# A depthwise and involution kernel: earlier prologue jobs, spare identity products on TensorE, fewer mirror DMAs and a last quarter summed in PSUM

## What is computed

```python
def _gn(v, G=32):                 # groups of two neighbouring channels: mean 0, variance 1
    ...
def _L0_conv_ref(x, ...):         # x is _gn(x)
    h = sign(x)
    h = depthwise_conv3x3(h, sign(dw_weight))
    h = sign(_bn(_prelu(h, prelu1_a), ...))
    h = einsum('bchw,oc->bohw', h, sign(pw_weight))
    return _bn(_prelu(h, prelu2_a), ...) + x
def _L1_conv_ref(x, W, b):        # x is _gn(x)
    filters = einsum('bchw,oc->bohw', x, W) + b      # 9 x 64 filters per pixel
    return sum over the 9 taps of (x shifted by the tap) * (its filter)
x = x + _L0_conv_ref(_gn(x), ...)
x = x + _L1_conv_ref(_gn(x), W, b)
```

## Time and profile before

| what | value |
|---|---|
| median of 3 runs | 772.26 us |
| the profiled execution, own time | 772.17 us |
| its span, first to last instruction | 770.3 us |
| VectorE (DVE) busy | 686.5 us, 89% |
| GpSimd (POOL) busy | 629.7 us, 82% |
| TensorE (PE) busy | 614.4 us, 80% |
| ScalarE (ACT) busy | 491.7 us, 64% |
| HBM read and written | 26.03 MB and 25.69 MB |

### The profile page before, as it was taken

How to read it: one execution, slowest core, us unless ns; L and a number is a source line. 1 busy time by engine, 2 the same in 40 slices (tenths; PEclk the granted TensorE clock), 3 DMA queues, 4 the chain that set the end, 5 groups by cost and what they waited for, 6 DMA issues and landing times.

```text
span 770.3 us, 18752 instructions
## 1 busy us (share of the span) xinstructions
PE 614.4 (80%) x7977; PEld 252.9 (33%) x7977; DVE 686.5 (89%) x988; ACT 491.7 (64%) x614; POOL 629.7 (82%) x421
## 2 busy tenths in 40 slices
PE   0628869888898989888898979888898988898880
PEld 0313324333342433343333423333333433332210
DVE  4346969999998989999998989999999989999998
ACT  5544877676857686776858586777868576725000
POOL 1030595989898898989899899989899899999996
PEclk9857999999999999999999999999999999999996
DMA  5206588898988889898988889898989887897982
GB/s 191 79 1 168 90 178 197 169 237 179 236 189 202 199 192 251 174 237 174 225 202 209 196 189 249 185 239 173 244 178 228 190 190 152 186 189 149 203 173 85
DMA packets 39683, 142.10 MB, mean 184 GB/s; under 512 B 4784, under 2 KB 12976, under 8 KB 37680
## 3 DMA queue, kind: packets, MB, share of 16 engines
q0 software_dynamic: 17136, 75.87, 53.6%
q1 hardware_dynamic: 22436, 65.04, 26.1%
q10 hardware_dynamic: 28, 0.00, 0.0%
HBM read 26.03 MB, written 25.69 MB: 67 GB/s over the span
## 4 chain that ended last, share of the span: by engine, by line
POOL 55%; DMA 19%; issue 9%; DVE 8%; ACT 4%; PE 4%; ACTq 1%; SPq 0%; POOLq 0%
DMA prod<-prod 18%; POOL prod L352 11%; POOL prod L346 11%; POOL ob L361 9%; POOL prod L319 6%; POOL prod L339 5%; POOL prod L331 4%; DVE prod L807 4%; POOL prod L328 4%; POOL st L306 2%; PE dw_ps L447 2%; ACT ab L497 1%; POOL st L304 1%; PE tap_ps L427 1%; ACT unused L497 1%
## 5 line engine op out<-in xcount | busy, mean ns | idle before, releaser
L427 PE MATMUL tap_ps<-q,w_t 64*64 64x392 f32 x2304 | 484.5, 509 | 51.8 <-DMA mirror<-q 20.4
L807 DVE SCALAR_TENSOR_TENSOR prod<-tap_ps,bias,q 128x784 f32<-128x784 f32 x480 | 474.6, 1026 | 35.4 <-PE tap_ps L427 32.9
L427 PE MATMUL tap_ps<-mirror,w_t 64*64 64x392 f32 x2304 | 478.2, 509 | 0.0
L427 PEld LDWEIGHTS tap_ps<-q,w_t 64*64 64x64 f32 x2304 | 149.3, 133 | 271.7 <-DVE prod L807 184.5
L497 ACT ACTIVATE ab<-dw_ps,col 128x784 bf16<-128x784 f32 x128 | 121.0, 995 | 97.7 <-PE dw_ps L447 97.7
L346 POOL TENSOR_TENSOR prod<-prod 128x784 f32<-128x784 f32 x63 | 135.4, 2150 | 9.1 <-DMA prod<-prod 9.1
L361 POOL TENSOR_TENSOR ob<-prod 128x784 f32<-128x784 f32 x63 | 142.2, 2258 | 0.2 <-POOL prod L352 0.2
L447 PE MATMUL dw_ps<-signs,dw_diag 64*64 64x392 bf16 x2304 | 134.8, 337 | 8.5 <-ACT ab L497 8.5
L427 PEld LDWEIGHTS tap_ps<-mirror,w_t 64*64 64x64 f32 x2304 | 136.2, 133 | 0.4 <-issue 0.4
L319 POOL DMA_DIRECT2D prod<-prod x63 | 80.5, 1278 | 65.1 <-DVE prod L807 64.8
L352 POOL TENSOR_TENSOR prod<-prod 128x784 f32<-128x784 f32 x63 | 132.9, 2110 | 0.0
(11 more groups left out here) (111 smaller groups left out, 443.5 us busy)
## 6 DMA issues: line engine op xcount, KB each, us to landing
prod<-prod POOLq DMA_DIRECT2D x63, 1176.0 KB, 10.6
out_dram<-ob SPq DMA_DIRECT2D x64, 392.0 KB, 7.6
xb<-in_x_dram SPq DMA_DIRECT2D x15, 1568.0 KB, 9.5
mirror<-q SPq DMA_DIRECT2D x128, 101.5 KB, 2.4
xb<-in_x_dram SPq DMA_DIRECT2D x2, 784.0 KB, 5.7
prod<-in_L_conv_W_dram SPq DMA_DIRECT2D x1, 288.0 KB
prm_rows<-in_L_conv_prelu_a_dram ACTq DMA_DIRECT2D x2, 0.5 KB
prm_rows<-in_L_conv_bn_var_dram SPq DMA_DIRECT2D x2, 0.5 KB
```

Source lines behind the costliest of these rows:

```text
L427: mm = pe.matmul(rows3(tap_ps[to, slot, side, 0:CH]), w_t[own, k, :], moving, start=True, stop=True)
L807: v.scalar_tensor_tensor(place.rearrange("p j (a b) -> p j a b", b=WD), psum.rearrange("p j (a b) -> p j a b", b=WD), s_(t, B4) if k == 4 ...
```

## The change

Its parts, in the order of the program:

1. **Parameter rows.** Three of the ten are issued by GpSimd, ahead of the instructions that make its identities; SP issues one and ScalarE six.
2. **Constants.** On VectorE `mean0` of tile 0 comes ahead of the nine diagonals, which now raise a semaphore of their own (`diag_ready`). TensorE's small product with `pw_k` moves from ahead of the first depthwise job to the first `pointwise`.
3. **Tile 0's jobs.** Jobs 1 and 3 put their depthwise sums in a slot of `tap_ps` in place of `dw_ps` (`in_ring`), and jobs 0 and 1 stand closer together.
4. **Tile 1.** Its squares are summed in four pieces between tile 0's jobs (`square_piece`), not in one after them; its signs are written in two parts.
5. **Spare products.** TensorE multiplies the 128 x 128 float32 identity by itself 12 times at the start, 16 times ahead of the first depthwise and 40 times between `turn_w` and the first taps. Nobody reads the result.
6. **Mirror.** Two DMAs for each half of a tile in place of four, each with the bytes of two.
7. **Last quarter.** It becomes one with `pair`; TensorE adds its planes 0 to 5 in `dw_ps` with the identity (`add_to_last`), and VectorE adds planes 6 and 7 in two instructions. The four additions L829 to L837 go.
8. **Places.** Some numbers of the tables change, among them `MEAN_DELAY` from 9 to 11 and tile 2's jobs by one to four units.

```diff
@@ parameter rows, POOL
             pool.memset(pw_block[:], 0.0).then_inc(half_ready, 1)
+            for n, v in ((0, a1), (7, bet2), (8, mu2)):
+                row(pool, n, v, rows_too)
@@ mirror_half, SP
-                    for qq in range(half * 2, half * 2 + 2):
-                        first = (2 * qq + side) * ROWS + 1
-                        sp.dma_start(mirror[own, t.par, qq, :, :], q[other, t.par, first:first + ROWS, :]).then_inc(mirrored[half], 16)
+                    of_quarters = q[other, t.par, 1:1 + H, :].rearrange("p (q s r) w -> p q s r w", s=2, r=ROWS)
+                    sp.dma_start(mirror[own, t.par, 2 * half:2 * half + 2, :, :],
+                                 of_quarters[:, 2 * half:2 * half + 2, side, :, :]).then_inc(mirrored[half], 16)
@@ PE
+            def keep_busy(slot, times):
+                for _ in range(times):
+                    pe.matmul(tap_ps[:, slot, 0, 0:P], ident_f32[:], ident_f32[:], start=True, stop=True)
+            def add_to_last(k):
+                g = TILES * QUARTERS - 1
+                pe.wait_ge(ab_done, TILES * JOBS)
+                pe.wait_ge(prod_done, KK * g + k + 1)
+                for half in range(2):
+                    mm = pe.matmul(dw_ps[:, half, 0:CH], ident_f32[:], prod[:, g % BUFS, k, half * CH:half * CH + CH],
+                                   start=(k == 0), stop=(k == PAIR_K - 3))
+                if k == PAIR_K - 3:
+                    mm.then_inc(last_added, 1)
...
             def depthwise(t, j, taps):
...
+                    if in_ring(t, j):
+                        wait_slot("dw", j)
+                    else:
+                        wait(pe, ab_done, j - 1 if t.first else t.count(JOBS, j))
...
+            keep_busy(1, BUSY[1])
+            pe.wait_ge(diag_ready, 1)
             for g in units:
                 if once("turn_w", g):
                     turn_w()
+                    pe.wait_ge(x1_done, JOBS)
+                    keep_busy(slots["tap", 2][0], BUSY[2])
                 for t, u in taps(g):
                     unit(t, u)
+                    if t.last and u in ADD_TO_LAST:
+                        for k in ADD_TO_LAST[u]:
+                            add_to_last(k)
@@ DVE
+            def square_piece(t, n):
+                piece = centred[:, n * QP:(n + 1) * QP]
+                then(v.tensor_scalar(piece, xb[:, t.x_slot, n * QP:(n + 1) * QP], s_(t, NM0), None, ALU.add))
+                v.scalar_tensor_tensor(piece, piece, 1.0, piece, ALU.mult, ALU.mult,
+                                       accum_out=squares[:, n:n + 1]).then_inc(squared, 1)
...
             def last_quarter(t):
-                v.tensor_tensor(pr[:, 0:3, :], pr[:, 0:3, :], pr[:, 3:6, :], ALU.add).then_inc(last_summed, 1)
...
+                v.scalar_tensor_tensor(two_banks, two_banks, 0.0, six, ALU.add, ALU.add).then_inc(last_summed, 1)
...
+                v.scalar_tensor_tensor(ob[:, ob_n, :].rearrange("p (j n) -> p j n", j=2), two_banks, 0.0, seven,
+                                       ALU.add, ALU.add).then_inc(last_summed, 1)
@@ tables
+BUSY = 12, 16, 40
+ADD_TO_LAST = {30: (0,), 31: (1,), 32: (2,), 35: (3, 4, 5)}
-MEAN_DELAY = 9
+MEAN_DELAY = 11
```

More of the change, by code:

```diff
@@ L105, in preact_involution_kernel @@
         scaled = sb("scaled", [P, JOBS], F32)
+        squares = sb("squares", [P, JOBS], F32)
+        scaled_squares = sb("scaled_squares", [P, JOBS], F32)
         def c_(n):
@@ L192, in on_pool, with pooled, kept, in_ring @@
         def on_pool(g):
-            return g % 2 == 1
+            return g % 2 == 1 and g < (TILES - 1) * QUARTERS
+        def pooled(g):
+            return sum(on_pool(n) for n in range(g + 1))
+        def kept(g):
+            return g + 1 - pooled(g)
         def planes(g):
             return [prod[:, g % BUFS, n, :] for n in range(PLANES)]
+        def in_ring(t, j):
+            return t.first and j % 2 == 1
+        def dw_banks(t, j):
+            return tap_ps[:, slots["dw", j][0], :, :] if in_ring(t, j) else dw_ps[:, :, :]
         def slots_in_turn():
@@ L201, in slots_in_turn @@
             for g in units:
+                for t, j in jobs(g, AB_DELAY):
+                    if in_ring(t, j):
+                        freed["dw", j] = len(freed)
                 for t, j in jobs(g, X1_DELAY):
@@ L210, in slots_in_turn @@
             for g in units:
-                uses = [("tap", g) for _ in taps(g)] + [("job", t.count(JOBS, j)) for t, j in jobs(g, PW_DELAY)]
+                uses = [("dw", j) for t, j in jobs(g, 0) if in_ring(t, j)] + [("tap", g) for _ in taps(g)] + [("job", t.count(JOBS, j)) for t, j in jobs(g, PW_DELAY)]
                 for use in uses:
@@ L234, in _ @@
         def _(sp):
-            for n, v in ((1, gam1), (4, var1), (9, var2)):
-                row(sp, n, v)
+            row(sp, 4, var1)
             sp.dma_start(dw_raw, dw.rearrange("c a i j -> c (a i j)").unsqueeze(0).broadcast_to([2, C, KK])).then_inc(signed_in, 16)
@@ L382, in _ @@
             pe.matmul(tap_ps[:, 2, 0, P:2 * P], pw_block[:], ident_sg[:], start=True, stop=True).then_inc(pw_turned, 1)
-            pe.wait_ge(pwk_ready, 1)
-            pe.matmul(tap_ps[:, 2, 1, 0:1], pw_k[:], minus_k_terms[:], start=True, stop=True).then_inc(k_ready, 1)
             def turn_w():
@@ L403, in wait_slot @@
                 was, n = before
-                if was == "job":
+                if was == "dw":
+                    pe.wait_ge(ab_done, n + 1)
+                elif was == "job":
                     pe.wait_ge(x1_done, n + 1)
                 elif n % KK == PAIR_K and not on_pool(n // KK):
-                    pe.wait_ge(paired, n // KK // 2 + 1)
+                    pe.wait_ge(paired, kept(n // KK))
                 else:
@@ L455, in pointwise @@
                 if t.first and j == 0:
+                    pe.wait_ge(pwk_ready, 1)
+                    pe.matmul(tap_ps[:, 2, 1, 0:1], pw_k[:], minus_k_terms[:], start=True, stop=True).then_inc(k_ready, 1)
                     pe.wait_ge(consts_ready, 1)
@@ L643, in _ @@
                         q_half(t, half)
+                if once("signs_rest", g):
+                    signs_second(30, H)
                 for t in tiles("inverse", g, 1):
@@ L709, in _ @@
             dve.wait_ge(act_set, 1)
+            mean0(Tile(0))
             for k in range(KK):
-                v.tensor_scalar(dw_diag[:, k, :], ident[:], dws[:, k:k + 1], None, ALU.mult)
-            mean0(Tile(0))
+                last = v.tensor_scalar(dw_diag[:, k, :], ident[:], dws[:, k:k + 1], None, ALU.mult)
+            last.then_inc(diag_ready, 1)
             dve.wait_ge(rs_ready, 1)
@@ L846, in _ @@
                     x1_sum(t, j)
+                for n in range(JOBS):
+                    if once(f"square_{n}", g):
+                        square_piece(Tile(1), n)
                 for t, u in taps(g):
@@ L938 @@
      'ratio': -45,
-     'job0': -43,
-     'job1': -38,
-     'job2': -33,
-     'job3': -28},
-}
-PROLOGUE = {"bias": -58, "turn_w": -47, "copy_w": -46}
+     'job0': -42,
+     'job1': -37,
+     'job2': -31,
+     'job3': -24},
+}
+PROLOGUE = {
+    'bias': -50,
+ 'turn_w': -46,
+ 'copy_w': -45,
+ 'signs_rest': -43,
+ 'square_0': -56,
+ 'square_1': -53,
+ 'square_2': -50,
+ 'square_3': -47,
+}
 AB_DELAY = 2
 RELU_DELAY = 6
+BUSY = 12, 16, 40
+ADD_TO_LAST = {30: (0,), 31: (1,), 32: (2,), 35: (3, 4, 5)}
 PW_DELAY = 5
```

97 lines of the change are left out of this document (52 added, 45 removed).

## The result

The changed kernel takes 744.97 us, the median of 4 runs (742.7 to 747.31), against 773.0 us for the kernel before on the same chip: a ratio of 0.965, 95% interval 0.960 to 0.970, so 28 us faster. The forecast was 38 us less, 734. The profiled execution of the changed kernel took 747.31 us, its span is 745.5; against the 770.3 of before that is 24.8 us less.

A forecast was written before the change was run, and what follows sets the result against it. The prediction took VectorE to set the steady pace, with GpSimd and the DMAs close behind. Its terms summed to -38.1 us, and 770.3 - 38.1 + 1.9 gave 734 us; range 722 to 747.

The forecast's parts named there:

- rival (1): Steady part: GpSimd or the fold's DMA sets the pace, or the mirror stays late; 744 us, chance 0.17.
- Tile 0's jobs: Prologue: sums start with the diagonals, jobs 1 and 3 get their own place; -8.5 us, far end -5.
- Tile 1's squares: Prologue: squares in pieces no longer stretch GpSimd's two small steps for tile 0; -4.6 us.
- Mirror before the first taps: Ahead of the first taps: two issues per half for four bring each half sooner; -0.9 us.
- First taps: Tile 0: 40 spare products raise TensorE's clock, so the taps begin at 2.4 GHz; -1.6 us, 0 to -2.5.
- Rival (2): Before the first taps: spare products run late at half clock; 739 us, or 745 with weight loads, chance 0.10.
- Tile 1's start: TensorE's waits of 3.20 us for ScalarE's reads and 2.27 for mirror pieces shrink; -3.8 us, 0 to -5.5.
- Steady part: Tile starts: VectorE's sixteen waits for taps shrink by 0.8 us each through an earlier mirror, 14 tiles; -11.2 us.
- The end: Last quarter: TensorE's plane additions replace VectorE's four, TensorE's lead hiding some 3 us; -7.5 us, -5 to -8.7.
- (3): Tile starts: the merged mirror piece lands late, deciding from about 5.2 us on; 808 us, slower, chance 0.03.
- (4): Prologue: ScalarE still waits job by job, -5 in place of -8.5 us; 741 us, chance 0.10.
- (5): Whole kernel: every boundary wait and the small waits inside tiles go too; 724 us, chance 0.05.

The follow-up runs named there:

- e11: Changed kernel with tile 0's jobs all in `dw_ps` one behind the other and tile 1's squares in one piece; 758.26 us, ratio 0.982.
- e5: Changed kernel without any spare products; 746.08 us, ratio 0.966.
- e6: Changed kernel without the last 40 spare products, the first 28 kept; 748.92 us, ratio 0.969.
- e1: Changed kernel with each mirror half in four DMAs again, as in the kernel before; 757.15 us, ratio 0.982.
- e9: Kernel of e1 with the load of x moved behind the next store; 745.15 us, ratio 0.965.
- e2: Kernel before with the merged mirror pieces alone; 763.42 us, ratio 0.990.
- e10: Changed kernel with the load of x moved behind the next store; 744.68 us, ratio 0.964.
- e4: Changed kernel with job 1 three units later in the steady table (-43 for -46); 744.19 us, ratio 0.966.
- e8: Changed kernel with `scales0` at -58, `q0` at -10 and `MEAN_DELAY` at 9, as in the kernel before; 743.91 us, ratio 0.962.
- e7: Changed kernel with the kernel before's end: VectorE's four additions instead of TensorE's plane additions and VectorE's two; 750.52 us, ratio 0.971.

## Why the prediction was right and where it was wrong

*The sign and the size.* The measured time lies in the range, at its upper end, and 11 us above the forecast. It is inside because the range left room for rival (1), not because the sum was right: the first two terms came whole, those behind them came out smaller, and the largest one failed. The time came out at rival (1)'s figure, 744. That rival named GpSimd or the fold's DMA as what sets the steady pace, and the DMA part of it was the real one, though not as it was put: not by its share of work in every tile, but by one collision with the load of x.

*Tile 0's jobs, -8.5:* right. The last `x1_sum` ended at 34.65 (forecast 35.2, before 43.7), -9.0; e11 shows that the ring's places, with job 1's nearer one, carry it.

*Tile 1's squares, -4.6:* right in size, 11.2 to 6.6 between the last `x1_sum` and `q`. e11 splits it: 2.2 for the pieces, the rest for the order in which the steps stand. The sum of tile 1 beside GpSimd's steps cost nothing (L735 above, with steps of 0.30 and 0.56). By the Trainium skill ("SBUF — State Buffer", Who interferes with whom) that instruction leaves GpSimd's ports alone; the trace agrees.

*Mirror before the first taps, -0.9:* mis-sized, -0.1. The piece was taken to land in 2.8 us; the median landing is 4.4. By the Trainium skill ("DMA: Bandwidth & Descriptors", Anatomy of one DMA) a DMA issued by GpSimd costs some 2.0 us plus its bytes over 436 GB/s, an estimate of 2.5 us for 203 KB. These pieces are issued by SP among other traffic, for which that fit isn't made; what counts here is the 4.4 us measured.

*First taps, -1.6, and spare products:* right in kind, taps at clock 1.00, first product at 48.12 (forecast 47.7). Rival (2) did not occur; the 40 products took 10.5 us, 0.26 each between the 0.22 and 0.43 of full and half clock, and ended 1.4 us before the first tap. What the first 28 were to bring shows nowhere (e5, e6). By the Trainium skill ("TensorE: Matmul & The Clock Gate", The HAM clock gate) a dense start earns the full rate as it goes on, and the trace agrees: 1.00 against e5's 0.69.

*Tile 1's start, -3.8:* the mirror, the first taps and this were forecast at 6.3 together and measured at 5.1. TensorE's 2.27 us for the mirror went as forecast, through the merged pieces (e1 and e9 have the wait again), but it still stood 2.2 us for ScalarE's reads.

*Steady part, -11.2:* wrong, -1.7 in the profiled execution. The step that failed is "sixteen waits of 17.1 us shrink by 0.8 each as the mirror comes sooner". In the trace of before each of the 13 tiles has its wait at the first unit, from 0.78 to 2.41 us, 16.2 us in all with two short ones behind the earlier trace rows. But it is made of two parts. The first is 0.8 us in every tile: TensorE stands for ScalarE's signs behind `q`, and no mirror touches that (e2 and e10 keep it, e4 removes it). The rest, 16.2 - 13 x 0.8 = 5.8 us, comes from the late fold by way of GpSimd. In the three tiles whose addition L346 had not waited for a fold the wait is 0.78, 0.80 and 0.80 us; the longest wait for a fold stands 20 us ahead of a `q` whose tile then waits 1.94, as GpSimd takes up the variance 2.0 us after VectorE's shuffle in place of 0.9:

```profile
432.17 1.87 POOL L346 TENSOR_TENSOR prod<-prod 128x784 f32<-128x784 f32 x1 [1.66 <-DMA prod<-prod]
...
458.52 1.97 DVE L807 SCALAR_TENSOR_TENSOR prod<-tap_ps,bias,q 128x784 f32<-128x784 f32 x2 [1.94 <-PE tap_ps L427]
```

(In the changed kernel such a delay shows in the middle of a tile, as at 289.81 us under theory D; in e8, with the three old numbers, at the first unit again, 2.3 us at most.) In the tile with 2.41 a lower clock adds to it: TensorE had stood 2.04 us for the signs, and its next matmuls last 0.86 us in place of 0.49. The whole that the change could win in the steady part without touching ScalarE's order was thus about 6 us, not 11.2, and it got part of it. TensorE's own waits in the trace of before would have told; over the 13 tiles it stood 25 times for ScalarE's signs and never for the mirror:

```profile
PE tap_ps L464 <- ACT ab L497: 37.3, 25, 2.6
```

*The end, -7.5:* mis-sized, -4.4 by the traces and 5.5 by e7. The step that failed is "of which its lead over VectorE hides some 3": it hid nearly nothing, VectorE waited 3.1 us. That is the sign of being wrong that the prediction had named, a wait of more than 2 us in the last quarter. The planes cost 1.4 to 1.6 us, not 1.3. GpSimd's last addition took 1.85 us and ended at 739.7, before VectorE's at 742.7, so it did not set the end as the prediction had it. The last `ob` is ready 4.5 us after the last product (13.6 before); the prediction's sign had "near 8 us", its own sum 758.8 - 753.9 = 4.9.

Rivals (3), (4) and (5) did not occur: the mirror's landing of 4.4 us is longer than taken and under the 5.2 that decides (3), and the jobs came whole. Of the other signs, the first wait of each tile was to be under 0.4 us and is 0.57 to 0.91 in the 13 tiles.
